# Scatter targets, slot list and token mixing moved to other places in a one-core mixture-of-experts and recurrence kernel

## The reference: what is computed

```python
x = x + _L0_ffn_ref(_L0_cond_ref(cond_1024, x, L0_cond_W, L0_cond_b, L0_cond_alpha), L0_ffn_W_A, L0_ffn_W_B, L0_ffn_W_up, L0_ffn_W_down)
x = x + _L1_ffn_ref(_L1_cond_ref(x, cond_1024, L1_cond_Wx, L1_cond_Wh, L1_cond_b), L1_ffn_w1, L1_ffn_w2)
```

## Time and profile before

| what | value |
|---|---|
| median of 3 runs | 373.31 us (371.96 to 375.29) |
| the profiled execution | 373.6 us, of which the span from first to last instruction is 371.9 us |
| busy in the span | PE 323.2, DVE 249.5, ACT 230.6, POOL 198.1 us |
| mean granted TensorE clock | 0.967 of 2.4 GHz |
| chain that ended last | PE 52%, DVE 8%, ACT 4%, DMA 3%, POOL 1% of the span |

### The profile page before, as it was taken

The page is one execution under the profiler, slowest core; times in us unless marked ns, Lnnn a source line. Parts: engine busy times, 40 slices in busy tenths (PEclk is TensorE's granted clock), DMA queues, the critical chain, the costliest instruction groups (busy, mean ns, idle before and its releaser), DMA issues.

```text
span 371.9 us, 11733 instructions
## 1 busy us (share of the span) xinstructions
PE 323.2 (87%) x3815; PEld 227.9 (61%) x3816; DVE 249.5 (67%) x823; ACT 230.6 (62%) x692; POOL 198.1 (53%) x212
## 2 busy tenths in 40 slices
PE   2587777777887999999899999999998899999973
PEld 2354444444554467767577777777777678888842
DVE  5556666768897768568446664443445899999774
ACT  2356665665556755555455565656565879999981
POOL 5648999999694445355645555555331233322230
PEclk9999999997588799999999999999999999999999
DMA  8993164681113478874344544544212213220001
GB/s 226 204 402 123 44 246 117 259 298 59 42 44 113 144 266 262 263 250 151 115 123 158 155 149 127 159 149 155 85 58 86 87 40 122 71 85 29 31 31 56
DMA packets 24272, 51.90 MB, mean 140 GB/s; under 512 B 3466, under 2 KB 16266, under 8 KB 23340
## 3 DMA queue, kind: packets, MB, share of 16 engines
q0 software_dynamic: 5824, 28.84, 24.1%
q1 hardware_dynamic: 18136, 22.59, 19.3%
q10 hardware_dynamic: 276, 0.01, 0.0%
HBM read 37.92 MB, written 13.50 MB: 138 GB/s over the span
## 4 chain that ended last, share of the span: by engine, by line
PE 52%; DVE 8%; ACT 4%; issue 3%; DMA 3%; POOL 1%; DVEq 0%; SPq 0%; POOLq 0%; ACTq 0%
PE bank L1062 13%; PE bank L1038 12%; PE bank L1025 5%; PE bank L1050 4%; PE bank L1197 3%; PE bank L1015 2%; PE bank L855 2%; PE bank L1167 2%; PE bank L862 1%; DVE peak L1739 1%; DMA z_hi<-token_rows,row_of_slot 1%; DMA y_rows<-z_lo,row_of_y 1%; PE bank L888 1%; PE bank L1176 1%; DVE wrec L1688 1%
## 5 line engine op out<-in xcount | busy, mean ns | idle before, releaser
L1580 DVE TENSOR_TENSOR wrec<-bank,wrec 128x512 f16<-128x512 f32 x39 | 27.0, 692 | 63.3 <-ACT wrec L702 63.3
L855 PEld LDWEIGHTS bank<-h_hi,wrec_hi 128*128 128x128 f16 x512 | 34.0, 97 | 52.9 <-ACT h_hi L660 47.0
L855 PE MATMUL bank<-h_hi,wrec_hi 128*128 128x32 f16 x512 | 43.6, 180 | 25.5 <-ACT h_hi L660 23.7
L562 POOL DMA_INDIRECT y_rows<-z_lo,row_of_y x39 | 38.2, 980 | 51.2 <-ACT z_lo L696 49.5
L1038 PE MATMUL bank<-wup_s,xgt 128*128 x234 | 63.2, 381 | 0.4 <-issue 0.4
L1062 PE MATMUL bank<-wdn_s,wrec 128*128 x468 | 58.0, 273 | 0.3 <-ACT wrec L702 0.3
L1062 PEld LDWEIGHTS bank<-wdn_s,wrec 128*128 128x128 f16 x468 | 44.8, 97 | 15.0 <-issue 1.9
L544 POOL DMA_INDIRECT z_hi<-token_rows,row_of_slot x37 | 36.3, 982 | 31.5 <-issue 17.1
L696 ACT ACTIVATE z_lo<-bank 128x256 f32<-128x256 f32 x39 | 14.9, 383 | 44.3 <-PE bank L1062 44.3
L855 PE MATMUL bank<-h_hi,wrec_lo 128*128 128x32 f16 x512 | 42.2, 178 | 0.0
L1324 DVE TENSOR_TENSOR_SCAN bank<-bank,terms 128x128 f32<-128x128 f32 x64 | 27.6, 431 | 17.6 <-ACT bank L656 14.7
(11 more groups left out here) (266 smaller groups left out, 900.4 us busy)
## 6 DMA issues: line engine op xcount, KB each, us to landing
stage<-wup POOLq DMA_DIRECT2D x2, 2048.0 KB, 10.9
token_rows<-ga_s SPq DMA_DIRECT2D x16, 256.0 KB, 3.1
stage<-wdn POOLq DMA_DIRECT2D x2, 2048.0 KB, 9.5
z_lo<-y_rows SPq DMA_DIRECT2D x32, 128.0 KB, 2.2
stage<-wb SPq DMA_DIRECT2D x2, 1024.0 KB, 12.5
token_rows<-hs_out SPq DMA_DIRECT2D x16, 128.0 KB, 2.6
stage<-w SPq DMA_DIRECT2D x4, 512.0 KB, 4.5
stage<-x_tm SPq DMA_DIRECT2D x4, 512.0 KB, 4.3
```

The costliest lines, as they stand in the source:

```text
L562: pool.indirect_dma_start(out=y_dram[:, :], in_=y_sb[j % 4][:, :], in_offset=None, out_offset=bass.IndirectOffsetOnAxis(ap=row_of_y[:, j:j ...
L855: mm(fm(par)[:, ft, cols], w[:, m, kt, fcols], h_hi[pp][:, kt, pcols], start=False, stop=True, skip_group_check=True)
L1580: ve.tensor_tensor(act_t[:, 1, :, :].rearrange("p k t -> p (k t)"), bank[(7, 3)[par]][:, :], act_t[:, 0, :, :].rearrange("p k t -> p (k t) ...
```

## The change

Three things move. No amount of TensorE or ScalarE work changes.

1. `targets(FIRST, STILES)` leaves GpSimd. VectorE does it as four operations of 128x28 (`targets_late`) after its expert tile 12, and GpSimd waits for the new semaphore `s_target` after gather 16, ahead of scatter 11.
2. `list_of(1, 1)` moves to the head of TensorE's expert tile 7, and `list_rows(1, 1)` ahead of VectorE's expert tile 7.
3. In `tanh_tile` for k = 2 to 5 the mixing of token tiles 4 to 7, and in part of 8, stands at other steps, and GpSimd's `x1_high` of token tile 7 stands ahead of its `quantise_hidden` of token tile 2 and not behind it.

```diff
-            def targets(first, end):
-                of = slice(first, end)
+            def targets_early():
+                of = slice(0, FIRST)
...
+                if j == FIRST + 5:
+                    pool.wait_ge(s_target, 1)
                 if j > FIRST + 1:
                     scatter_y(j - 5)
-                if j == FIRST + 4:
-                    targets(FIRST, STILES)
...
             def tanh_tile(k, par):
+                if k == 5:
+                    x1_high(7, 1)
                 if live(k - 3, TILES - 1):
                     quantise_hidden(k - 3, 1 - par)
-                for t in ((3, 4) if k == 2 else (k + 2,) if k in (3, 4) else (7, 8) if k == 5 else (k + 3,) if k > 5 else ()):
+                for t in ((3, 4) if k == 2 else (k + 2,) if k in (3, 4) else (k + 3,) if k > 4 else ()):
...
             def expert_tile(j, par, expert, c, word_of=None):
+                if isinstance(j, int) and j == 7:
+                    list_of(1, 1)
...
-                    if j == 7:
-                        list_of(1, 1)
...
+            def targets_late():
+                of = slice(FIRST, STILES)
+                ve.tensor_scalar(size[:, of], signed_row[:, of], 0.0, float(NTOK), ALU.is_lt, ALU.mult)
+                link(ve.scalar_tensor_tensor(target[:, of], signed_row[:, of], 0.0, spare_row[:, of], ALU.is_equal, ALU.mult))
+                link(ve.tensor_tensor(target[:, of], target[:, of], size[:, of], ALU.add))
+                ve.tensor_tensor(row_of_y[:, of], target[:, of], row_of_slot[:, of], ALU.add).then_inc(s_target, 1)
...
+            list_rows(1, 1)
             expert_tile(7, 1)
-            list_rows(1, 1)
             list_words(1)
...
+                if m == 3:
+                    targets_late()
...
                     if s == 0:
                         if at == 2:
                             combine_second(3, 1)
+                        if at in (3, 4):
+                            combine_first(k + 2, par)
+                        if at == 5:
+                            combine_second(7, 1)
                         if live(k - 3):
                             quantiser_hidden(k - 3, 1 - par)
...
-                        if at == 4:
-                            combine_first(6, 0)
-                        if at == 5:
-                            combine_second(7, 1)
...
-                        if at in (0, 3):
+                        if at == 0:
                             combine_first(k + 2, par)
                             combine_second(k + 2, par)
-                        if at == 4:
-                            combine_second(6, 0)
+                        if at == 2:
+                            combine_first(4, 0)
...
-                        if at in (0, 3, 4):
                             x1_low(k + 2, par)
+                        if at in (2, 3, 4):
+                            combine_second(k + 2, par)
...
-                        if at == 2:
-                            combine_first(4, 0)
-                            combine_second(4, 0)
...
-                        if at == 2:
-                            x1_low(4, 0)
+                        if at in (2, 3, 4):
+                            x1_low(k + 2, par)
```

More of the change, by code:

```diff
@@ L288, in adaln_ffn @@
         s_empty = sem("s_empty")
+        s_target = sem("s_target")
         s_tanh = sem("s_tanh")
@@ L569, in _ @@
                 if j == 3:
-                    targets(0, FIRST)
+                    targets_early()
                 if j >= 5:
```

## The result

| what | before | after |
|---|---|---|
| median | 373.17 us (371.96 to 377.26, 13 runs) | 370.87 us (369.38 to 372.47, 13 runs) |
| profiled execution, span | 373.6, 371.9 us | 370.83, 369.0 us |
| ratio of after to before | | 0.9918, 95% interval 0.9896 to 0.994 |

The ratio is 3.06 us off 373.17, with 2.2 to 3.9 us as its interval: faster, and a little less than 1%. The forecast was 369.8 (368.7 to 371.8).

What follows compares the result with a forecast made beforehand. The prediction took TensorE to bound the kernel for most of the span, with stalls at the three edits. Terms 1.70 + 0.65 + 1.2 = 3.55 us off the median 373.31 gave 369.8 us, range 368.7 to 371.8.

Steps and rivals of the forecast that it cites:

- What bounds it: Waits run through TensorE for most of the span; busy 92.70 of 93.00 us from 185 us, it carries earlier gains whole.
- Edit 1: Expert tile 14: moving the targets lets gather 16 start on time, 5.45 to 3.75 us, -1.70 us.
- The rival of a new wait: Late targets, semaphore or gathers from 16 on replace the target stall; 1.70 not won, 371.5 us, chance 0.09.
- The cost of 0: VectorE's added 0.9 us fits in 1.28 us idle; the wait ahead of scatter 11 has 1.1 us to spare.
- Edit 2: Expert tile 9: the earlier list lets gather 11 start at 156.7, 4.40 to 3.75 us, -0.65 us.
- the price of 0: Expert tile 7: moved list products cost TensorE nothing new; list copies fit in VectorE's 3.05 us idle before 155.50.
- Edit 3: Tanh tiles 2 to 5: three VectorE stalls totalling 1.71 us go, part stays as other waits, -1.2 us.
- the sign of error: Prediction is wrong if TensorE in tanh tiles 3 to 5 waits for the quantised rows in place of `h_lo`.
- The mixing without gain: Rival: recurrence round trip or later quantisation replaces the three mixing stalls; 2.35 us remain, 371.0 us, chance 0.17.
- all that fits (2.1): Rival: VectorE's lateness was the mixing's only limit, so 2.1 us instead of 1.2; 368.9 us, chance 0.10.
- The steady tiles: Rival: tanh tiles 6 to 15 each collide with the quantisation, costing 4.0 to 7.9 us; 373.8 to 377.7, chance 0.04.

Runs made afterwards that it cites:

- targets only: The kernel before with only the late scatter targets moved to VectorE and the wait ahead of scatter 11; 372.35 us, ratio 0.9958.
- experiment 8: Changed kernel with VectorE's four target operations one expert tile later, behind its tile 13 (also called Targets one tile later); one execution at 374.57 us.
- after again: The changed kernel, unaltered, measured a second time; 369.69 us over 6 runs, ratio 0.9878 to the kernel before.
- the kernel without the list: Changed kernel with the list move undone, targets and mixing still moved; 372.98 us, ratio 0.9962 to the kernel before.
- mixing only: Changed kernel with the target and list moves undone, so only the mixing is moved; 372.08 us, ratio 0.9951 to the kernel before.

## Why the prediction was right, point by point

- **What bounds it, and that a gain made before 185 us is carried.** Right. From the `down` at the end of tile 15 to `h_lo` of tanh tile 0 are 89.76 us before (188.79 to 278.55) and 89.76 after (186.40 to 276.16). So TensorE, full there, kept the whole gain.
- **Edit 1, -1.70.** Measured -1.67 in after, and 1.65 between before and targets only. The gap of 0.80 was half of the loss, as said: tile 14 returned to the distance of an undisturbed one. The weight loads had waited 1.29, so the gather was wanted at 182.12 and not at 182.61, and the room was 1.0 us at worst and not 1.5; it sufficed. Gather 16 was forecast at 175.6 and came at 175.54. The rival of a new wait is refuted where the change put it; experiment 8 shows where it begins, one tile later. A gather of this stretch took up to 5.5 us to land instead of 4.9 (median 4.0 in both), and it met enough slack. The cost of 0 for what the edit adds was right where the prediction looked, in the expert stage, and wrong at the end: about 0.3 us in `tanh_tile(12)` and behind the last operation come with it in every profile.
- **Edit 2, -0.65.** -0.77 in the pair of profiles, 0.65 at the median of the kernels. Gather 11 was forecast at 156.7 and came at 156.44. I had looked at tile 9 alone; tile 10 gives another 0.12, and tile 9 itself is anything from 3.97 to 4.40 with the list in its old place. Here the price of 0 holds only for VectorE. On TensorE the list costs 0.03 to 0.04 us in tile 7 (3.84 instead of 3.80 or 3.81).
- **Edit 3, -1.2.** Measured -1.26. The parts were off by up to 0.2 and cancelled, so that the sum fits this well is luck: tile 2 -0.12 (0.1 said), tile 3 -0.35 (0.3), tile 4 -0.64 (0.45), tile 5 -0.15 (0.35). In tile 4 the prediction gave the collision too little (0.63 of its 0.79 were on the path) and the wait something, where it was worth nothing. In tile 5 the 0.38 us in which TensorE waited for `h_lo` went, and the 0.35 for `z_lo` came. That is near the sign of error that the prediction named, TensorE waiting for something else in place of `h_lo`, though not for the quantised rows.
- **The rivals.** The mixing without gain, and all that fits (2.1), are refuted by 1.14 us in tiles 3 to 5. The steady tiles don't collide: tanh tiles 6 and 7 are 4.70 and 4.72 us where they were 4.69 and 4.73, and 8 to 14 are equal within 0.01 us but for tile 12 (0.08).
- **The size.** The three terms in the two profiles are 0.77 + 1.67 + 1.26 = 3.70 us against 3.55 said. The first measurement gave 2.2 to 3.9 us and the second 374.09 x (1 - 0.9878) = 4.6 (3.4 to 5.8). What kept the first median 1.1 above the forecast is not a term of the sum: the profile, which lies at that median, has 0.45 us in expert tiles 7 and 8, 0.43 in tanh tile 1 and 0.32 behind `h_lo` of tile 6. The first doesn't come back in after again. The second does with 0.34, because the profile of before was a lucky one there: tanh tile 1 has 3.83 to 4.53 us in the twelve, and 3.87 in before. The third comes back whole and is the price of edit 1 at the end. The second median, 369.69, hits the forecast, and the first misses it by 1.1: both are of one kernel. The prediction had given the median of a few runs half a microsecond, and two of them lie 1.2 apart.

## What to carry to other kernels

Work that sits in a queue ahead of a transfer costs only what is left of it when the idle time that it fills and the slack of that transfer are taken off: the same 3 us of GpSimd cost 1.67 us ahead of gather 16 and 0.2 us behind it. Read from PEld and not from PE when a tile was wanted: the weight loads waited 1.29 and 0.71 us where the products waited 0.80 and 0.22. Read what a stall costs from the distance of equal products around it, then check the neighbouring tile as well. On an engine that is late, walk the distances of the recurrence step by step: a collision cost 0.61 to 0.63 of its 0.76 to 0.79 us, while a wait of 0.46 in the same tile cost nothing, since the next step was shorter by as much. And look for what the moved operation now stands ahead of: `combine_second(7)` lost 0.35 us that way.

## What the hardware did that I had not expected

TensorE's granted clock fell to 0.50 ahead of the last products in three of the twelve profiles, near places where TensorE had stood still. Windows of the kernel without the list (stretch, its length, busy PE, PEld, DVE, ACT, POOL, PEclk, DMA share, GB/s):

```profile
355.00:360.00 5.00, 4.06 (x37) 2.34 (x36) 3.97 (x15) 4.27 (x8) 1.98 (x2) 1.00 0.16 52
363.00:366.00 3.00, 2.15 (x15) 1.46 (x12) 0.74 (x2) 0.60 (x1) 0.00 (x0) 0.50 0.13 44
```

Its TensorE timeline from there, and behind it that of after:

```profile
362.46 0.98 PE L1200 MATMUL bank<-w_q,z 128*128 128x256 f16 x4 [1.92 <-DVE z_lo L1784]
...
366.22 1.87 PE L1200 MATMUL bank<-w_q,z 128*128 128x256 f16 x8 [1.07 <-DVE z_lo L1784]
```
```profile
362.42 0.60 PE L1200 MATMUL bank<-w_q,z 128*128 128x256 f16 x4 [1.93 <-DVE z_lo L1784]
...
364.97 1.03 PE L1200 MATMUL bank<-w_q,z 128*128 128x256 f16 x8 [1.07 <-DVE z_lo L1784]
```

The same products take 1.87 us at 1.2 GHz and 1.03 us at 2.4, and from the first of these rows to the end are 371.1 - 362.46 = 8.6 us instead of 369.0 - 362.42 = 6.6. The waits ahead of them are equal, 1.92 and 1.93, then 1.07 us in both, so the wait alone doesn't decide it. Targets only has the same at 364 us. Targets one tile later has it in the tail, and also at the change of stages:

```profile
284.00:288.00 4.00, 3.42 (x65) 2.43 (x62) 2.02 (x7) 2.19 (x10) 0.40 (x1) 1.00 0.46 131
289.50:293.00 3.50, 3.49 (x42) 2.99 (x43) 2.94 (x12) 2.35 (x8) 0.41 (x1) 0.52 0.29 80
```

There TensorE is full and at half clock, and tanh tiles 2 and 3 are 0.61 and 0.63 us longer, in that profile alone. Nothing in that kernel's edit lies near 290 us.

The first stage, ahead of all moved work, has the low clock in every one of the twelve, between 87 and 105 us and again between 118 and 127. In after it is (windows, as above):

```profile
90.00:100.00 10.00, 8.47 (x98) 5.14 (x96) 8.16 (x38) 4.89 (x21) 6.85 (x6) 0.50 0.15 55
```

In after the first fall lasts about 17 us, in mixing only about 3.5. With it go the mean clocks of before and after, the lowest of all (0.967 and 0.966), though neither has a fall ahead of the last products. What it costs there isn't shown: the first `down` product starts at 130.63 to 133.06 us in the twelve, and the latest isn't the one with the longest fall. So a mean clock of the whole span tells little here.

What makes the clock fall in one execution and not in the next stays open. Ahead of the last products or at 290 us it is worth 1 to 2 us, as much as any edit of this change, and a reader who compared two single executions of this kernel would read it as the change's doing.
